# Six changes of queue order in a four-layer attention and feed-forward kernel

## The reference

```python
x = x + L0_xattn(layernorm(x), ctx, mask, ...)    # 32 blocks of 128 columns, 8 heads; Gelu of the output; projection
x = x + L0_ffn(layernorm(x), ...)                 # softmax router over 8 low-rank pairs A, B (rank 16)
x = x + L1_xattn(layernorm(x), ctx, ...)          # top-k channels of the context, max and mean, conv, gate
x = x + L1_ffn(layernorm(x), ...)                 # base matmul + 8 low-rank experts, top 2 of a softmax router
x = x + L2_xattn(layernorm(x), ctx, ctx, ...)     # 32 heads, 8 key/value heads of width 16, softmax
x = x + L2_ffn(layernorm(x), ...)                 # (silu(x Wg) * (x Wu)) Wd, width 1376
x = x + L3_xattn(layernorm(x), ctx, ctx, pos, causal_mask, ...)
#   q, k rotated by position; 32 heads, 8 key/value heads, of width 128; softmax(q k / sqrt(128)) v; Wo
x = x + L3_ffn(layernorm(x), up, down, perm)
#   columns permuted; 16 heads: gelu(t[32] @ up[32, 128]) @ down[128, 32]; permuted back
```

## Time and profile before

| | |
|---|---|
| time, 3 executions | 1481.80, 1480.16, 1479.09 us, median 1480.16 |
| profiled execution | 1477.75 us, span 1475.9 us, 20655 instructions |
| granted TensorE clock, mean over the span | 0.961 of 2.4 GHz |
| PE busy | 1328.7 us (90%), weight loads 1003.5 (68%) |
| DVE busy | 956.7 us (65%) |
| ACT busy | 595.0 us (40%) |
| POOL busy | 549.8 us (37%) |
| chain of waits that ended last | PE 62%, DVE 17%, issue 7%, POOL 6%, ACT 4%, DMA 3% |

### The profile page before, as it was taken

The page is one execution under the profiler, slowest core; times in us unless marked ns, Lnnn a source line. Parts: engine busy times, 40 slices in busy tenths (PEclk is TensorE's granted clock), DMA queues, the critical chain, the costliest instruction groups (busy, mean ns, idle before and its releaser), DMA issues.

```text
span 1475.9 us, 20655 instructions
## 1 busy us (share of the span) xinstructions
PE 1328.7 (90%) x6958; PEld 1003.5 (68%) x6958; DVE 956.7 (65%) x2109; ACT 595.0 (40%) x1609; POOL 549.8 (37%) x548
## 2 busy tenths in 40 slices
PE   2887868888898999999999879999999999999687
PEld 1554544666677776777878767777787777776465
DVE  6999955587533588842222556776777777777654
ACT  2787773362312345443121224344343444434341
POOL 5001014542313335142221444464454545444184
PEclk9999987998997999999999999999999999999999
DMA  5211101321121001021110131011120111110001
GB/s 166 58 35 39 30 16 57 108 65 65 65 79 50 1 8 30 1 91 50 40 56 22 54 110 38 30 58 51 36 83 33 58 51 36 51 58 8 0 1 58
DMA packets 53609, 71.68 MB, mean 49 GB/s; under 512 B 5935, under 2 KB 24688, under 8 KB 53506
## 3 DMA queue, kind: packets, MB, share of 16 engines
q1 hardware_dynamic: 52592, 69.15, 14.9%
q10 hardware_dynamic: 914, 1.22, 0.3%
HBM read 55.67 MB, written 10.49 MB: 45 GB/s over the span
## 4 chain that ended last, share of the span: by engine, by line
PE 62%; DVE 17%; issue 7%; POOL 6%; ACT 4%; DMA 3%; SPq 1%; POOLq 0%; DVEq 0%; ACTq 0%
PE bank L411 15%; PE bank L416 14%; PE bank L415 14%; PE bank L2382 3%; DVE topv L1588 2%; PE bank L2264 2%; POOL ring_l L1029 2%; PE bank L2360 2%; PE bank L2246 2%; DVE top L1582 2%; PE bank L2369 1%; DVE bank L1874 1%; POOL probs L1176 1%; DVE xn L1848 1%; DVE xn L1834 1%
## 5 line engine op out<-in xcount | busy, mean ns | idle before, releaser
L1029 POOL TENSOR_TENSOR ring_l<-stage,ring_h 128x512 fp32r<-128x512 f32 x137 | 182.2, 1348 | 230.4 <-ACT ring_h L1206 230.3
L411 PE MATMUL bank<-xTh_b,ring_h 128*128 128x512 f32 x464 | 190.1, 410 | 2.9 <-POOL ring_l L1029 1.4
L415 PE MATMUL bank<-xTl_b,ring_h 128*128 128x512 f32 x464 | 184.3, 397 | 0.0
L416 PE MATMUL bank<-xTh_b,ring_l 128*128 128x512 f32 x464 | 184.2, 397 | 0.0
L1151 POOL TENSOR_TENSOR q<-xn 128x512 f32<-128x512 f32 x64 | 82.2, 1285 | 207.2 <-DVE xn L1848 207.2
L411 PE MATMUL bank<-ring_h,o3h 128*128 128x512 f32 x256 | 125.7, 491 | 1.2 <-issue 1.1
L1495 ACT ACTIVATE probsT<-bank 128x512 f32<-128x512 f32 x64 | 38.3, 599 | 201.7 <-PE bank L2369 201.7
L1507 ACT ACTIVATE probs<-bank,nbias 128x128 f32<-128x128 f32 x256 | 90.7, 367 | 53.2 <-DVE nbias L1876 53.2
L411 PEld LDWEIGHTS bank<-xTh_b,ring_h 128*128 128x128 f32 x464 | 88.1, 190 | 23.5 <-issue 4.3
L416 PEld LDWEIGHTS bank<-xTh_b,ring_l 128*128 128x128 f32 x464 | 87.7, 189 | 21.5
L416 PE MATMUL bank<-ring_h,o3l 128*128 128x512 f32 x256 | 101.4, 396 | 0.0
(11 more groups left out here) (331 smaller groups left out, 3267.8 us busy)
## 6 DMA issues: line engine op xcount, KB each, us to landing
stage<-in_units_dram SPq DMA_DIRECT2D x137, 256.0 KB, 3.1
ring_l<-k SPq DMA_DIRECT2D x64, 64.0 KB, 2.0
raw_k<-kvs SPq DMA_DIRECT2D x16, 256.0 KB, 2.0
kraw<-raw_k SPq DMA_DIRECT2D x16, 256.0 KB, 3.4
v<-raw_v SPq DMA_DIRECT2D x16, 256.0 KB, 2.9
stage<-in_context_dram SPq DMA_DIRECT2D x8, 256.0 KB, 2.9
raw_v<-kvs SPq DMA_DIRECT2D x8, 256.0 KB, 2.0
out_dram<-X SPq DMA_DIRECT2D x8, 256.0 KB, 2.0
```

The costliest lines, as they stand in the source:

```text
L411: ins = nc.tensor.matmul(out_ap, wh, mh, start=start, stop=False)
L415: nc.tensor.matmul(out_ap, wh, ml, start=False, stop=False)
L416: return nc.tensor.matmul(out_ap, wl, mh, start=False, stop=stop)
L1029: nc.gpsimd.tensor_tensor(ring_l[:, place_of(u), :], stage[:, u % STAGE, :], f32(ring_h[:, place_of(u), :]), ALU.subtract).then_inc(w_lo, 1)
```

## The change

Six places, all of them the order of work on the queues. No product, no tile and no number of the result is changed.

1. **Context at once.** SyncE waits for the last products of the first attention (a0_pv) in place of the residual sums (x_done), and then loads all four chunks. Chunks 2 and 3 get the buffers cosT and sinT, each chunk has a semaphore of its own. ScalarE's four context_hi stand together ahead of the router. Unit 4 is split under the softmax and the following ones after the router.
2. **Units of the third attention.** ScalarE splits 3 units, then has four ln_act, 2 units, four ln_act, and 5 units. Before it was 10 units and then eight ln_act.
3. **Query piece.** In the last attention the projection queries3(6) stands before the first turn of probabilities, and before it stood behind it.
4. **Statistics.** ln_one, ln_row and ln_low of the last layer norm stand behind the work on the softmax in VectorE's rows 59 to 67, and before they stood ahead of it.
5. **Tables.** table_for() is an activation of one column, [128, 1], into wr, a tile that is no longer read. It stands at five places: Gelu and Exp around the Gelu of the first attention, Silu ahead of the third attention's last part, Exp after the first units of the last attention, Gelu after the last unit. There are still 6 table loads.
6. **Third tile.** tile_hi(2) and tile_lo(2) of the last feed-forward stand behind the second Gelu (and behind its high part on VectorE). Before they stood ahead of the first.

```diff
@@ SyncE
-            sp.wait_ge(x_done, XD_L0A + B)
+            sp.wait_ge(a0_pv, 4 * G0)
...
-                if k >= 2:
-                    sp.wait_ge(c_lo, k - 1)
-                nc.sync.dma_start(chunk(k), d["contextT"][k]).then_inc(s_ctxT[k % 2], 16)
+                nc.sync.dma_start(chunk(k), d["contextT"][k]).then_inc(s_ctxT[k], 16)
...
-            context_load(0)
-            context_load(1)
+            for k in range(KT):
+                context_load(k)
             load.upto(5)
-            context_load(2)
-            context_load(3)
@@ ScalarE
+        def table_for(func):
+            i = next(table)
+            nc.scalar.activation(wr[:, 0, i:i + 1], ident[:, 0:1], func)
...
+            table_for(ACT.Gelu)
             for j in range(2):
                 a.wait_ge(a0_po, B * j + B)
                 nc.scalar.activation(oN[:, 4 * j:4 * j + 4, :, 0:64], oN[:, 4 * j:4 * j + 4, :, 0:64], ACT.Gelu).then_inc(o0_g, 1)
+            table_for(ACT.Exp)
...
-            context_hi(0)
-            context_hi(1)
+            for k in range(KT):
+                context_hi(k)
             def under_softmax():
-                context_hi(2)
-                context_hi(3)
-                hi.upto(5)
+                hi.upto(4)
             router_act(a, 0, under_softmax, 4)
+            hi.upto(5)
             hi.upto(7)
...
             hi.upto(U_L2X + 3)
+            ln_act(a, LN_L2X[1], xTh_b, 4)
+            hi.upto(U_L2X + 5)
+            ln_act(a, LN_L2X[1], xTh_b, 8, 4)
             hi.upto(U_L2X + 10)
-            ln_act(a, LN_L2X[1], xTh_b)
...
+            table_for(ACT.Silu)
             for q in range(4):
                 kv_act(a, 25 + q)
...
             hi.upto(U_L3X + 3)
+            table_for(ACT.Exp)
...
             hi.upto(N_UNITS)
+            table_for(ACT.Gelu)
             ln_act(a, LN_L3F[1], xTh_b, B, 2)
...
-            for n in range(3):
+            for n in range(2):
                 tile_hi(n)
...
                 nc.scalar.activation(gel[n % 4], bank[n % 4][:], ACT.Gelu).then_inc(z_g, 1)
+                if n == 1:
+                    tile_hi(2)
@@ VectorE
-                    if m >= 56:
-                        ln_one(v, LN_L3F[0], m - 56)
-                if n >= 64 and n < 68:
-                    ln_row(v, *LN_L3F, n - 60)
-                if n >= 63:
-                    ln_low(v, LN_L3F[1], n - 63, xTh_b, xTl_b)
...
+                if 59 <= n < 67:
+                    ln_one(v, LN_L3F[0], n - 59)
...
-                if 60 <= n < 64:
+                if 60 <= n < 68:
                     ln_row(v, *LN_L3F, n - 60)
+                if n >= 63:
+                    ln_low(v, LN_L3F[1], n - 63, xTh_b, xTl_b)
@@ TensorE
+                if n == 1:
+                    queries3(6)
                 if 0 <= m < 64:
...
-                if n + 5 < 64:
+                if n != 1 and n + 5 < 64:
                     queries3(n + 5)
```

More of the change, by code:

```diff
@@ L12 @@
 from concourse.alu_op_type import AluOpType as ALU
+import itertools
 import numpy as np
@@ L385, in program @@
         s_unit = [sem(f"s_unit{i}") for i in range(STAGE)]
-        s_ctxT = [sem(f"s_ctxT{i}") for i in range(2)]
+        s_ctxT = [sem(f"s_ctxT{i}") for i in range(KT)]
         s_out = sem("s_out")
@@ L503, in ln_pe @@
                     then(b)
+        table = itertools.count()
+        def table_for(func):
+            i = next(table)
+            nc.scalar.activation(wr[:, 0, i:i + 1], ident[:, 0:1], func)
         def ln_act(a, n, th, upto=B, first=0):
@@ L810, in chunk @@
         def chunk(k):
-            return (probs, probsT)[k % 2][:, 0:2, :].rearrange("p a f -> p (a f)")
+            if k >= 2:
+                return (cosT, sinT)[k % 2][:, :]
+            return (probs, probsT)[k][:, 0:2, :].rearrange("p a f -> p (a f)")
         a2_pj = sem("a2_pj")
@@ L1931, in _ @@
                 nc.vector.tensor_copy(gel_h[n % 4], gel[n % 4]).then_inc(z_gh, 1)
+                if n == 1:
+                    tile_lo(2)
                 if n % 4 == 0 and 1 <= n // 4 < 6:
```

4 lines of the change are left out of this document (2 added, 2 removed).

## The result

The changed kernel takes 1460.45 us (median of four executions, 1458.42 to 1461.52) beside 1479.62 us for the kernel before (four, 1476.74 to 1481.80). The ratio is 0.987, with a 95% interval of 0.9849 to 0.9891: 19.2 us less. The forecast was 1459.2 us and 21.0 us less, so the direction and the sum held.

What follows compares the result with a forecast made beforehand. TensorE, busy 90% of the span, was taken as the bound. Savings of 3.0 + 9.5 + 2.3 + 0.2 + 0.1 + 5.9 = 21.0 us from 1480.16 gave 1459.2 us (0.986), range 1452.5 to 1467.5.

Steps and rivals of the forecast that it cites:

- Context: Before the key projections: wait falls from 3.47 to 1.2 us at full clock; 3.0 us less kept at the channel attention.
- Units: Third attention: earlier value projection saves 4.55 us and half clock 7.25, less a new query wait; net 9.5 us less.
- The new wait: Third attention: five splits before the first query copy make TensorE wait 2.3 us for the query low part.
- Query piece: Last attention's start: projection of piece 6 fills the 6.71 us idle before the first transposes; 2.3 us less.
- 2.3 are saved: Last attention: second transposes at 892.77 had probabilities ready at 890.47, so they could come 2.3 us sooner.
- Statistics: Rows 59 to 63 of the last attention: transposes come earlier, VectorE's residual sum stays; 0.2 us less, between 0 and 2.2.
- Tables and the third tile: Earlier tables 0.1 us less; last feed-forward 5.9 less: 4.0 from the first down projection's wait, 1.9 from half clock.
- Half clock stays: Rival: shortened gaps still drop the clock in the third attention and before key projections; 12.2 us saved, 1468; chance 0.14.
- own sign of being wrong: Half clock behind the gaps the change shortens, or a longer row period in the last attention, would make the forecast wrong.
- More than the sum: Rival: no new wait in the query loop, last attention gains 1.0 more; 24.5 us saved, 1455.5; chance 0.14.
- The gain given back: Rival: unit 4's late split cancels 3.0, last feed-forward gains only the load's 1.3; 13.4 us saved, 1466.8; chance 0.08.
- the slower kernel: Rival: moving piece 6 makes every last-attention row wait more; at 0.5 us a row 31 lost, 1490; chance 0.03.

Runs made afterwards that it cites:

- x_l2: Changed kernel, with the third attention's last five unit splits moved one by one behind the first five query copies: 1457.48 us, 0.9825 of the kernel before.
- x_both: Changed kernel with later unit splits in the third attention and, on ScalarE and GpSimd, in the last attention: 1450.95 us, 0.9786 of the kernel before.
- p3_piece: Kernel before, with only the projection queries3(6) moved ahead of the last attention's first turns: ratio 1.0001 (0.9990 to 1.0012).
- x_l3: Changed kernel, with the last attention's four output units split behind the first row's exponentials, low parts behind the second row's probabilities: 1455.40 us, 0.9812 of the kernel before.
- p4_stats: Kernel before, with only the last layer norm's statistics moved behind VectorE's softmax work: ratio 1.0012 (0.9996 to 1.0027).
- p6_tail: Kernel before, with only Gelu's table ahead of the last layer norm and the third tile behind the second Gelu: ratio 0.9970 (0.9949 to 0.9990).
- p6_tile: Kernel before, with only the last feed-forward's third tile moved behind the second Gelu: ratio 0.9984 (0.9965 to 1.0003).

## Why the prediction was right, point by point

- **The sum.** Forecast were 21.0 us less. In the medians it is 19.2 in the first comparison and 25.0 in the second, in the two traces 16.2 and 21.4. Behind the first 223 us, which scatter, the traces have 19.0 and 21.7 less. The terms from the traces are 3.5 for the context, 8.5 for the units, 0.7 to 2.2 for the piece, 0.5 for the tables, 7.4 from the first up projection to the end, and between 1.3 gained and 0.2 lost from 904 to there; 1.5 are lost again in the third attention. The mechanisms were right in the main. That the sum came so close is in part luck: the units and the piece gave less than forecast, 1.5 us went at a wait that the change does not touch, and the end gave 1.5 more than forecast by a half clock that the prediction had not looked at.
- **Context, 3.0 forecast, 3.5 measured.** Each step held: the wait (1.2 forecast, 1.16 measured), the full clock behind it, the slack of 0.4 us at the tables, the roots 3 us sooner.
- **Units, 9.5 forecast, 8.5 measured.** The mechanism held, and what it saves was 11.8 in the forecast and 12.0 in x_l2 and x_both, which lack the new wait. The new wait was 1.80 us (2.3 forecast), but with its clock it took 3.5 in place of 2.3. The term that was mis-sized is this one: a wait on TensorE was priced for the half clock that goes with it, at 7.25 us here and 1.6 there, and not for the half clock that comes with a new one. The 1.7 us of half clock behind the 1.80 us were left out.
- **Query piece, 2.3 forecast, 0.7 to 2.2 in traces, no difference in the medians.** The step that failed is "2.3 are saved", read from the probabilities being ready 2.3 us ahead of the second turns. The second turns did come sooner after the first ones, by 1.9 and 2.1 us in the two traces of the changed kernel and 1.4 in p3_piece. But the half clock did not go with the moved matmuls: where it lasted 6.8 us it lay on whatever came next. The forecast's lower end for this term, 1.0, was put down to just that, and is nearer to what three of four traces show (0.7 to 0.8, with x_l2).
- **Statistics, 0.2 forecast.** 1.2 to 1.3 us less or 0.1 to 0.2 more in traces with the edit, not told apart from nothing by the medians. The waits moved from the turns to the output projections.
- **Tables and the third tile, 6.0 forecast, 7.4 at the end and 0.5 before it in traces.** The wait held: 0.82 us where 0.7 was forecast, 3.9 us gone where 4.0 was. The half clock had 1.9 and gave 3.5, of which some 1.5 lie at the other wait of 1.50 us. The medians of the part alone have 4.4 less (1.5 to 7.6). The Trainium skill's page "ScalarE: Activation LUTs", section "What ACT_TABLE_LOAD costs", has a drain of some 1.38 us beside the load. No trace here shows it: the table alone took 1.4 us from the wait, about the load's 1.28 us.
- **The rivals.** "Half clock stays" did not come true where it was priced. The Trainium skill's page "TensorE: Matmul & The Clock Gate", section "Part 4: PE-mode transpose", says that a transpose does not count as busy in the same way. Here, with gaps of 1.07 and 0.43 us between these turns, the clock was 1.00 from 440 to 460. The prediction's own sign of being wrong, half clock behind these gaps, did appear behind two that it had made or left: the new query wait and the first turns of the last attention. "More than the sum" had no new wait; it came. (Its arithmetic is 21.0 + 2.3 + 1.0 = 24.3, not 24.5.) The gain given back fell, and so did the slower kernel: the last attention's rows take as long as before (0.4 to 0.5 us less in all from 904 to 1358).

## What to carry to other kernels

An engine that splits weights for later should not do so ahead of work that is waited for now: three of the four waits here were copies or subtractions of the future in front of one of the present, and x_l3, which took such work out of the way, was worth more than the edit that had tried to fill the same wait. In the fourteen traces, from 233 us on, all 35 waits of TensorE of 3.3 us and more were followed by half clock, for 3.4 us up to 20.5, and 69 of the 115 between 1.75 and 2.5 us (it began in the wait or within 4 us behind it). So price a wait with the clock behind it, the wait that an edit makes as well as the one that it takes away, and give the clock behind a wait near 2 us a chance and not a certainty. And compare traces instruction by instruction in the stretch of the edit; the ends of two traces differed here by 5 us for the same kernel.

## What was not expected of the hardware

**The same wait was followed by half clock in one execution and not in another.** At the end of the third attention TensorE waits 2.00 us for a low part of GpSimd, in every kernel and with the same instructions around it. Behind it, in the kernel before and in the changed kernel:

```profile
634.16:637.20 3.04, 3.04 (x13) 2.53 (x14) 1.34 (x4) 0.00 (x0) 2.44 (x8) 1.00 0.00 0
```

```profile
624.91 0.50 PE L413 MATMUL bank<-ring_h,onT_h 128*128 128x512 f32 x1 [2.00 <-POOL onT_l L1141]
...
624.91:628.00 3.09, 3.09 (x9) 2.48 (x10) 0.81 (x2) 0.65 (x2) 2.48 (x8) 0.64 0.00 0
```

13 matmuls at 1.00, and 9 at 0.64. It costs 1.5 us. By the time from there to 639, of the six traces with the split units five have it (not x_l2), of the eight others one (p4_stats). Something beyond the wait's length decides; what it is stays open.

**The first 223 us took between 1.6 us less and 5.0 us more than in the profiled execution of before**, in fourteen traces with the same code up to the last 10 us. The mean granted clock from 0 to 223 us was 0.88 in the slowest (p6_tail), 0.90 to 0.92 in the others and 0.93 in p6_tile, which was 0.2 us quicker; but x_l2, at 0.92 like the kernel before, was 3.6 us late, so the clock is not all of it. The traces don't tell what sets it off. It is a third of a per cent of the time, as much as some parts of this change are worth.
